# Routing a mixture of experts tile by tile: rows scattered to expert regions during attention instead of gathered by inverted tables behind it

## The reference

```python
h = x + _attention(_rmsnorm(x, g1), wq, wk, wv, wo)
xf = _rmsnorm(h, g2).reshape(-1, E)
probs = jax.nn.softmax(xf @ w_router, axis=-1)
topw, topi = jax.lax.top_k(probs, 2)
topw = topw / jnp.sum(topw, axis=-1, keepdims=True)
combine = jnp.sum(one_hot(topi, 8) * topw[..., None], axis=1)
g = silu(einsum('td,xdh->txh', xf, wg)); u = einsum('td,xdh->txh', xf, wu)
eo = einsum('txh,xhd->txd', g * u, wd)
y = h + einsum('txd,tx->td', eo, combine)
```

## Time and profile before

| | us |
|---|---|
| median of 3 runs (756.78 to 757.3) | 756.88 |
| the profiled execution: its own time | 758.17 |
| its span, first to last instruction | 756.4 |
| PE busy, of the span | 611.4 |
| DVE busy | 499.0 |
| ACT busy | 394.0 |
| POOL busy | 267.3 |

### The profile page before, as it was taken

The page is one execution under the profiler, slowest core; times in us unless marked ns, Lnnn a source line. Parts: engine busy times, 40 slices in busy tenths (PEclk is TensorE's granted clock), DMA queues, the critical chain, the costliest instruction groups (busy, mean ns, idle before and its releaser), DMA issues. The chain is left out here.

```text
span 756.4 us, 28418 instructions
## 1 busy us (share of the span) xinstructions
PE 611.4 (81%) x11893; PEld 460.5 (61%) x11893; DVE 499.0 (66%) x1131; ACT 394.0 (52%) x831; POOL 267.3 (35%) x391
## 2 busy tenths in 40 slices
PE   4788999999989989898898889841469998988840
PEld 2355666666656565656655555630369987988840
DVE  3377688778777777777777687838826654555437
ACT  3255466555455555454645444451537765655525
POOL 4010110101121321322314241222567777777750
PEclk9599999999999999999999999975569999999985
DMA  4304400001000010010100001010031111111129
GB/s 129 109 18 159 125 18 17 28 22 34 6 27 27 7 55 16 28 45 28 44 17 13 34 17 45 31 56 1 26 129 53 50 54 54 51 52 55 51 76 303
DMA packets 35246, 39.88 MB, mean 53 GB/s; under 512 B 10256, under 2 KB 25424, under 8 KB 34992
## 3 DMA queue, kind: packets, MB, share of 16 engines
q1 hardware_dynamic: 30576, 28.74, 11.8%
q0 software_dynamic: 4544, 9.32, 4.3%
HBM read 20.80 MB, written 10.94 MB: 42 GB/s over the span
## 5 line engine op out<-in xcount | busy, mean ns | idle before, releaser
L1209 DVE TENSOR_REDUCE rmax<-ps_s 128x16 f32<-128x1024 f32 x96 | 117.2, 1221 | 82.2 <-PE ps_s L1019 81.6
L1082 ACT ACTIVATE probsT<-ring 128x512 f32<-128x512 f32 x192 | 103.8, 591 | 100.6 <-PE ring L1031 100.6
L1213 DVE TENSOR_TENSOR shifted<-ps_s,rmax 128x1024 f32<-128x1024 f32 x96 | 117.6, 1225 | 10.2 <-PE ring L1047 0.5
L665 PE MATMUL ps_s<-room 128*128 128x128 f32 x852 | 110.3, 281 | 0.0
L1031 PE MATMUL ring<-const,shifted 128*128 128x128 f32 x768 | 106.5, 282 | 1.1 <-DVE att L1225 1.1
L665 PEld LDWEIGHTS ps_s<-room 128*128 128x128 f32 x852 | 104.0, 197 | 0.0
L743 DVE SCALAR_TENSOR_TENSOR room<-room,ps_s 128x384 f32<-128x384 f32 x71 | 39.3, 554 | 80.2 <-ACT room L715 80.2
L1047 PEld LDWEIGHTS ring<-vbd,probsT 128*32 128x32 f32 x6144 | 62.3, 110 | 44.1 <-issue 39.6
L1031 PEld LDWEIGHTS ring<-const,shifted 128*128 128x128 f32 x768 | 83.8, 142 | 5.4 <-issue 1.1
L1335 POOL TENSOR_TENSOR pt<-mv,small 128x4 f32<-128x4 f32 x24 | 4.8, 200 | 217.8 <-DVE mv L1238 217.8
L610 POOL DMA_INDIRECT room<-hn_dram,gather_rows x71 | 68.8, 969 | 28.9 <-issue 20.1
(11 more groups left out here) (172 smaller groups left out, 916.4 us busy)
## 6 DMA issues: line engine op xcount, KB each, us to landing
room<-kS SPq DMA_DIRECT2D x96, 64.0 KB, 1.9
room<-y_dram SPq DMA_DIRECT2D x16, 256.0 KB, 5.7
room<-in_x SPq DMA_DIRECT2D x8, 256.0 KB, 3.3
hn_dram<-hn SPq DMA_DIRECT2D x8, 256.0 KB, 2.3
base_dram<-base SPq DMA_DIRECT2D x8, 256.0 KB, 2.4
room<-base_dram SPq DMA_DIRECT2D x1, 2048.0 KB, 7.8
out<-room SPq DMA_DIRECT2D x8, 256.0 KB, 4.9
cin<-in_ctx SPq DMA_DIRECT2D x8, 192.0 KB, 2.9
```

The source lines that it names most:

```text
L665: last = mm(bank[r][:, k * P:(k + 1) * P], w, xbT[r], start=True, stop=True)
L1082: nc.scalar.activation(probsT[p % 2][:, 4 * g:4 * g + 4, :], ring[u.bank][:].rearrange("p (k c) -> p k c", c=P), ACT.Exp, scale=SCALE)\
L1209: V.reduce_max(rmax[p % 2][:].rearrange("p (g k) -> p g k", g=GROUPS), ps_s, AX.X).then_inc(rmax_ready, 1)
L1213: V.tensor_tensor(shifted[p % 2][:].rearrange("p (g k) s -> p g k s", g=GROUPS), ps_s, rmax[p % 2][:].rearrange("p (g k) -> p g k", g=GROU ...
```

## The change

- The choice and the ranking are done for each tile during attention. `lg` on DVE becomes `choose_dve`, one job behind it a new step `rk` ranks the tile's rows on PE (a strictly lower triangle of ones, and the counts carried over from earlier subtiles) and `place_dve` turns ranks into addresses. Each expert has a region of 33 blocks in `moved_dram`.
- Each row is written twice, once for each choice, as 130 floats: the row, the place in `y_dram` to which its result goes, and half its weight. Eight scatters of 128 rows for each tile (steps `s0` to `s3`, two each) do it on POOL. `export` is gone, and so is the inversion of the tables.
- The rows of a region are consecutive, so a block is loaded by one plain transfer from a base address. SP issues it, with the base from a `value_load`. It can be issued when the result of eight blocks earlier is stored, since the scatter takes its addresses from the same buffer. POOL only scatters results. The result is weighed as it is copied out (L752 in the numbering of before), so combining is two additions for each tile.
- Behind the last tile a block's unused rows are filled: SP stores 8 pad blocks at the ends of the regions; 7 dummy blocks are stored early. `tables_dve` works out expert and base of each block.
- `ap` moves from place 0 to place 1 of its slot, behind the exponentials; `xT` and `k` move on by one place. The sum `base` stays in `xs[t]`.

```diff
 STEPS = {
-    2: {SELF: (((), ("st",)), (("ap",), ()), (("xT",), ("k",)), ((), ())),
-        CROSS: (((), ("st",)), (("ap",), ("cT",)), ((), ("k",)), ((), ("xT",))),
-        ROTARY: (((), ("st",)), (("ap",), ()), (("xT",), ("k",)), (("kr",), ("ap3",)))},
+    2: {SELF: (((), ("st",)), ((), ("ap",)), ((), ("xT",)), (("k",), ())),
+        CROSS: (((), ("st",)), ((), ("ap", "cT")), ((), ("k",)), ((), ("xT",))),
+        ROTARY: (((), ("st",)), ((), ("ap",)), ((), ("xT",)), (("k",), ("kr", "ap3")))},
     1: {SELF: ((("q",), ("v",)), ((), ()), ((), ()), ((), ())),
         CROSS: ((("q",), ("v",)), ((), ()), ((), ()), ((), ())),
         ROTARY: ((("q",), ("qr",)), ((), ("v",)), ((), ()), ((), ()))},
...
          ROTARY: (((), ()), (("oT",), ("wo", "st2")), ((), ("ap2",)), ((), ("hT",)))},
     -2: {SELF: (((), ()), ((), ()), ((), ()), ((), ())),
          CROSS: (((), ()), ((), ()), ((), ()), ((), ())),
-         ROTARY: (((), ("lg",)), ((), ()), ((), ()), ((), ()))},
+         ROTARY: (((), ("lg",)), ((), ("rk",)), ((), ("s0",)), ((), ("s1",)))},
+    -3: {SELF: (((), ()), ((), ()), ((), ()), ((), ())),
+         CROSS: (((), ()), ((), ()), ((), ()), ((), ())),
+         ROTARY: (((), ()), ((), ("s2", "s3")), ((), ()), ((), ()))},
 }
-NOT_ON_PE = ("st", "ap", "ap3", "st2", "ap2")
+MOVES = ("s0", "s1", "s2", "s3")
+NOT_ON_PE = ("st", "ap", "ap3", "st2", "ap2") + MOVES
...
+    yield "lg", last - 1
+    yield "s2", last - 2
+    yield "s3", last - 2
+    yield "oT", last
+    yield "wo", last
+    yield "rk", last - 1
+    yield "st2", last
+    yield "ap2", last
+    for name in MOVES:
+        yield name, last - 1
+    for name in ("hT", "lg", "rk") + MOVES:
+        yield name, last
...
+    moved_dram = nc.dram_tensor("moved_dram", [(EXPERTS * REGION + DUMMIES) * P, ROW], F32).ap()
+    y_dram = nc.dram_tensor("y_dram", [2 * TOKENS + (EXPERTS + DUMMIES) * P, E], F32).ap()
...
+    def choose_dve(dve, n):
+
+        V, t, u = nc.vector, TILE_OF[n], used("lg", n)
+        iota = const[:, C_IOTA:C_IOTA + EXPERTS].unsqueeze(1).broadcast_to([P, SUB, EXPERTS])
+
+        def wide(x):
+            return x.unsqueeze(2).broadcast_to([P, SUB, EXPERTS])
+
+        dve.wait_ge(ring_filled, u.filled())
+        V.tensor_copy(logits[:], ring[u.bank][:, 0:SUB * EXPERTS].rearrange("p (s e) -> p s e", s=SUB))\
+         .then_inc(ring_drained[u.bank], 1)
+        dve.wait_ge(ring_drained[u.bank], u.drained())
+        for k, src in enumerate((logits, second)):
+            in_turn(dve, V.reduce_max(top[:, k, :], src[:], AX.X))
+            in_turn(dve, V.tensor_tensor(less[:], src[:], wide(top[:, k, :]), ALU.is_lt))
+            in_turn(dve, V.scalar_tensor_tensor(keyed[:], less[:], float(EXPERTS), iota, ALU.mult, ALU.add))
+            in_turn(dve, V.tensor_reduce(first_at[:, k, :], keyed[:], AX.X, ALU.min))
+            in_turn(dve, V.tensor_tensor(chosen[:, k], iota, wide(first_at[:, k, :]), ALU.is_equal))
+            if k == 0:
+                in_turn(dve, V.scalar_tensor_tensor(second[:], chosen[:, 0], -1e30, logits[:], ALU.mult, ALU.add))
+        wait(dve, weight_ready, t)
+        V.tensor_tensor(gap[:], top[:, 1, :], top[:, 0, :], ALU.subtract).then_inc(gap_ready, 1)
+        V.tensor_copy(carried[:, 0, :], region_at[:] if t == 0 else carried[:, SUB, :])
+        in_turn(dve, V.tensor_tensor(sel[:], chosen[:, 0], chosen[:, 1], ALU.add))
+        for s in range(SUB):
+            add = V.tensor_tensor(carried[:, s + 1, :], carried[:, s, :], sel[:, s, :], ALU.add)
+            if s < SUB - 1:
+                in_turn(dve, add)
+            else:
+                add.then_inc(sel_ready, 1)
+
+    def place_dve(dve, n):
+
+        V, t, u = nc.vector, TILE_OF[n], used("rk", n)
+        dve.wait_ge(ring_filled, u.filled())
+        rank = ring[u.bank][:, 0:SUB * EXPERTS].rearrange("p (s e) -> p s e", s=SUB)
+        if t == TILES - 1:
+            in_turn(dve, V.tensor_copy(last_row[:], ring[u.bank][:, SUB * EXPERTS:(SUB + 1) * EXPERTS]))
+        V.tensor_tensor(at_expert[:], chosen[:], rank.unsqueeze(1).broadcast_to([P, 2, SUB, EXPERTS]), ALU.mult)\
+         .then_inc(ring_drained[u.bank], 1)
+        dve.wait_ge(ring_drained[u.bank], u.drained())
+        in_turn(dve, V.reduce_sum(pos_f[:], at_expert[:], AX.X))
+        r = t % 2
+        wait(dve, rows_moved[r], MOVED * (t // 2))
+        V.tensor_copy(pos_i[r][:], pos_f[:])
+        rows = const[:, C_ROW:C_ROW + 2 * SUBS].rearrange("p (k s) -> p k s", k=2)[:, :, t * SUB:(t + 1) * SUB]
+        V.tensor_copy(moved[r][:].bitcast(I32)[:, :, :, E], rows)
+        dve.wait_ge(weight_ready, t + 1)
+        in_turn(dve, V.tensor_scalar(wsum[:], w1st[:], 2.0, 2.0, ALU.mult, ALU.add))
+        in_turn(dve, V.reciprocal(moved[r][:, 0, :, E + 1], wsum[:]))
+        V.tensor_tensor(moved[r][:, 1, :, E + 1], w1st[:], moved[r][:, 0, :, E + 1], ALU.mult).then_inc(rows_known, 1)
+
...
-        dve.wait_ge(rows_known, 1)
-        for c in range(CHOICES // CHUNK):
-            ms = range(c * CHUNK, (c + 1) * CHUNK)
-            if c < CHOICES // CHUNK // 2:
-                for m in ms:
-                    last = V.tensor_scalar(blk_hot[:, m, :], wide_b[:, 0:BLOCKS], blk_f[:, m:m + 1], None, ALU.is_equal)
-                last.then_inc(blocks_hot[c], 1)
-            for m in ms:
-                V.tensor_scalar(row_hot[:, m, :], wide_b[:], row_f[:, m:m + 1], None, ALU.is_equal)
-            dve.wait_ge(blocks_hot[c], 1)
-            V.tensor_scalar(blk_code[:, ms[0]:ms[-1] + 1, 0, :], blk_hot[:, ms[0]:ms[-1] + 1, :],
-                            const[:, C_COL:C_COL + 1], None, ALU.mult).then_inc(rows_hot, 1)
-
...
-        sp.wait_ge(exported, EXPORT * TILES)
-        sp.wait_ge(inverted, 1)
-        sp.dma_start(residual, base_dram).then_inc(base_loaded, 16)
+        sp.wait_ge(pads_known, 1)
+        for e in range(EXPERTS):
+            at = sp.value_load(pad_at[0:1, e:e + 1], min_val=0, max_val=(EXPERTS * REGION - 1) * P)
+            sp.dma_start(moved_dram[bass.ds(at, P), :], pads[:, e, :]).then_inc(pads_stored, 16)
+        sp.wait_ge(experts_known, 1)
+        for r in range(2):
+            sp.wait_ge(rows_moved[r], MOVED * TILES // 2)
+        sp.wait_ge(pads_stored, 16 * (EXPERTS + DUMMIES))
+        for j in range(USED):
+            r = j % UNROLL
+            if j >= UNROLL:
+                sp.wait_ge(y_stored[r], 16 * (j // UNROLL))
+            at = sp.value_load(base_at[0:1, j:j + 1], min_val=0, max_val=(EXPERTS * REGION + DUMMIES - 1) * P)
+            sp.dma_start(xb[r], moved_dram[bass.ds(at, P), :]).then_inc(xb_loaded[r], 16)
...
+        for j in range(USED):
+            r = j % UNROLL
+            pool.wait_ge(y_copied, j + 1)
             G.indirect_dma_start(out=y_dram, in_=yb[r], in_offset=None,
...
-        for c in range(UNROLL):
-            gather(0, c)
-
-        for j in range(USED):
-            i, c = divmod(j, UNROLL)
-            if there(i, c + UNROLL):
-                pool.wait_ge(xbT_filled, j + 1)
-                gather(i, c + UNROLL)
-            if there(i, c - 1):
-                pool.wait_ge(y_copied, j)
-                scatter(i, c - 1)
-        pool.wait_ge(y_copied, USED)
-        scatter(*divmod(USED - 1, UNROLL))
+                                 out_offset=bass.IndirectOffsetOnAxis(ap=xb[r].bitcast(I32)[:, E:E + 1], axis=0))\
+             .then_inc(y_stored[r], 16)
...
-            V.tensor_scalar(yb[r], y_bank[c % 2], 0.5, None, ALU.mult).then_inc(y_copied, 1)
+            V.tensor_scalar(yb[r], y_bank[c % 2], xb[r][:, E + 1:E + 2], None, ALU.mult).then_inc(y_copied, 1)
...
+            elif name == "rk":
+                rank = ps_g[:, 0:SUB * EXPERTS].rearrange("p (s e) -> p s e", s=SUB)
+                mm(rank, const[:, C_LOW:C_LOW + P], sel[:], start=True, stop=False)
+                last = mm(rank, ones[:], carried[:, 0:SUB, :], start=False, stop=True)
+                if t == TILES - 1:
+                    last = mm(ps_g[:, SUB * EXPERTS:(SUB + 1) * EXPERTS], ones[:], carried[:, SUB, :],
...
     def combine_dve(dve):
         V = nc.vector
-        dve.wait_ge(base_loaded, 16)
+        dve.wait_ge(base_ready, TILES)
         y0, y1 = y_both
         for t in range(TILES):
-            for s in range(t * SUB, (t + 1) * SUB):
-                if s % (SUBS // PARTS) == 0:
-                    dve.wait_ge(y_loaded[s // (SUBS // PARTS)], 32)
-                V.scalar_tensor_tensor(y0[:, s, :], y0[:, s, :], weight0[:, s:s + 1], residual[:, s, :],
-                                       ALU.mult, ALU.add).then_inc(first_added, 1)
-            dve.wait_ge(weighed, (t + 1) * SUB)
-            dve.wait_ge(first_added, (t + 1) * SUB)
             sl = slice(t * SUB, (t + 1) * SUB)
+            dve.wait_ge(y_loaded[t], 32)
+            V.tensor_tensor(y0[:, sl, :], y0[:, sl, :], residual[:, sl, :], ALU.add).then_inc(first_added, 1)
+            dve.wait_ge(first_added, t + 1)
```

(18 more changed lines are left out.)

316 lines of the change are left out of this document (107 added, 209 removed).

## The result

The changed kernel takes **749.44 us** (median of 4 runs, 748.21 to 752.07) against 756.83 before (median of 4, 755.98 to 757.3): a ratio of 0.9908, 95% interval 0.9884 to 0.9932. It is faster by 0.9%, where I had forecast 3.7% and a range that ended at 747. The profiled execution, the longest of the four, took 752.07 us, span 750.3.

What follows compares the result with a forecast made beforehand. Bounds: attention PE with DVE, routing a chain on DVE and neighbours, experts POOL's queue, combining DVE. +19 - 21.6 - 22.5 - 3.1 = -28.2 took the profiled 758.17 to 730.0, so 729 us predicted; 8-in-10 range 716 to 747.

Steps and rivals of the forecast that it cites:

- Routing, -21.6: Between attention and experts: POOL's 16 scatters end last, and PE's first transpose comes at 532.0 instead of 553.6.
- Experts, -22.5: Experts' stage: without gathers on POOL, PE's 2.12 us a block becomes the period; 158.2 us against 180.7.
- The third and fourth rival: Experts' stage: buffers come back late, 742 us, chance 0.12; SP's turn takes PE's place, 764 us, chance 0.07.
- Combining, -3.1: Last stage: DVE's two additions make 1.46 us a tile instead of 1.85, eight times 0.39 less.
- Attention, `ap` moved, -5: Attention: exponentials ahead of `ap` take back 5 of the 6.0 us that PE waits for a bank.
- Attention, POOL, 0: Attention: scatters on POOL cost nothing, since ACT's idle time covers most of the RMS norms' delay.
- Attention, choice and placing, +24: Attention: the choice on DVE makes output matmul and scores 4.0 us late, six times; placing runs under matmuls.
- The sum: Whole kernel: attention +19 (+24 - 5), routing -21.6, experts -22.5, combining -3.1, together -28.2 us.
- The second rival: Attention pays more (placing, late norms, little from `ap`): +8 to +14, 737 to 743 us; attention ends behind 522; chance 0.15.
- The first rival: Attention: small DVE instructions cost half, 0.1 us apiece, a tile delays by 2 not 4; 717 us, chance 0.15.

Runs made afterwards that it cites:

- e11: Changed kernel with half of every output store left out, so half of the rows aren't written: 747.29 us, ratio 0.9862.
- e5: Kernel before the change with only the new places of `ap`, `xT`, `k` and `kr`: 752.26 us, ratio 0.9891.
- e1: Changed kernel with all eight scatters of a tile moved so that none stands ahead of an RMS norm: 742.32 us, ratio 0.9759.
- e2: Changed kernel with `ap`, `xT`, `k` and `kr` back where they stood before: 752.58 us, ratio 0.9915.
- e9: Changed kernel with 14 matmuls whose results nobody reads added behind the ranking matmuls of six tiles: 743.37 us, ratio 0.981.
- e4: Changed kernel with 13 instructions of choice for 19, leaving ties between experts undecided: 740.53 us, ratio 0.9775.
- e7: Changed kernel with the choice cut in two blocks, the second round one place later, and ranking half a pair later: 735.53 us, ratio 0.9666.

## Why the prediction was wrong, step by step

- **Routing, -21.6: right** (-21.8). The steps came in the order forecast, POOL's 16 scatters last, a pitch of 1.26, a landing of 2.3; the first transpose is 31.9 behind the addition of `wo` (537.70 to 569.60), forecast 31.
- **Experts, -22.5: nearly right** (-20.6). 2.12 a block, SP's turn no bound, the buffers just in time. The mis-sized term is the last scatter, which I had at 2.4 "since no other is queued": another was queued, and the first `y` load starts 3.5 behind the last copied result. Another 0.7 lie in the 68 periods. The third and fourth rival did not happen.
- **Combining, -3.1: half** (-1.5). The mis-sized term is the end. DVE's two additions are 0.69 each, and from the first `y` load to the end of its last addition it took 15.7 where it took 19.4, a little more than I had forecast. But the faster DVE lets the stores start sooner on DMA engines that are still loading: the last store lands 4.9 after DVE's end (745.39 to 750.3), before it was 2.8 (753.64 to 756.4). e11 shows that the stores' traffic bounds it.
- **Attention, `ap` moved, -5: right** alone (-6.6 in e5).
- **Attention, POOL, 0: this step failed.** I had seen the pair `s2`, `s3` ahead of the norm and priced it at 0, "2 each" without cover. It cost 5.8 each, twice: 11.4 in the ladder's steps, 10.4 of attention given back by e1. The cover that I read in the earlier trace rows, ACT idle for 2.49 behind `hn`, was slack of ACT in the kernel before, and the change had put `xT` into it, which I had "cost at nothing". Two edits at nothing each, and together PE waited 4.79 and then lost 2.2 more at half clock. e2 shows that both were needed at these two places: with `xT` back, norms 2.05 and 2.07 late cost nothing there. It shows too that 0 would have been wrong all the same: a third norm, 3.98 late with `kS` behind it, cost 3.5. As a whole the old places gained nothing, since they gave up the 6.6 of the new ones.
- **Attention, choice and placing, +24: the delay was right, the clock behind it was left out.** 4.0 a tile is what a step costs when PE is kept busy (e9's first three: 3.8, 4.0, 3.9), and PE in job 16 started 3.9 late. In the changed kernel a step is 5.1 to 5.8: PE waits up to 3.5 and then runs the next matmuls at half clock. The three groups behind the wait in job 16 take 3.60 where 2.12 stood, 1.5 more, and the fillers gave 1.6 back in each of the first three steps, 8.3 in all.
- **The sum:** 24 (choice) + 9.3 (what e1's six steps, 33.3 in all, have above 24; the clock in the main) + 11.4 (norms) - 6.6 (places) = 38.1, measured 37.8. The second rival, attention pays more, had the sign and the place, and "behind 522" as its mark (534); it stopped at +14 because it too priced the late norms at most at 6 and had nothing of the clock.
- The first rival is dead: a small instruction is 0.19 and 0.22 from start to start. By the Trainium skill's 60 ns (Perfetto Trace Analysis, section Optimizing Scalar/DVE Operations) the choice would have taken about 1.8 us, my estimate. The same section puts the profiled latency at about twice the 60 ns, and in a chain where each instruction waits for the last it is the latency that counts: 2 x 60 and the 33 of data would give about 2.9, also an estimate. It took 3.74.

Open: in the two late norms (5.8 each) the rows give the clock 2.2, but no run took it out alone. Why e9's last step stays at 5.0 is not known, nor whether e4's gain is more than the 1.3 us that DVE gave up in each choice.

## What to carry to other kernels

Price a new block on an engine by three things: the delay of what stands behind it, what the delayed engine's queue holds behind that, and what PE's clock does after the wait. Two edits that each lean on the same slack are not each free; check the slack of the kernel after both. New work for DVE in a tight loop is better cut in pieces that stand ahead of different row maxima (e7, 6.0 us of attention), and a scatter's issue belongs behind a norm that another engine waits for: four ahead of one cost 5.8, or nothing, by what stood in the next queue.

## What I had not expected of the hardware

- PE at half clock behind waits of 2.0 to 3.5 us: the output matmuls take 1.81 to 2.05 us for 1.02 to 1.06, and from job 13 on the same work costs 13.4 us more. Twenty microseconds of useless matmuls in the waits buy 8.3.
- A chain of 128x32 DVE instructions has a pitch of 0.22 us, 0.19 of it busy, and even 128x4 ones take 0.16 to 0.18.
- A scatter of 128 rows costs POOL's queue 1.26 us, 0.96 of it busy, and lands 2.3 after its issue; beside the experts' loads one on the critical chain took 4.06.
- With all 16 DMA engines at 0.92 of their time the rate in combining was 305 GB/s; a store of 256 KB then lands 6.1 us after its issue (median).
